# A second attention whose query and output products become three products of rounded parts, with keys and values loaded batch by batch

## The chip, the cores and the metric

The kernel runs on one core of one Trainium2 chip. The metric is the device time of one execution, in microseconds. Before the change three runs took 3955.93 to 3960.25 us, with a median of 3957.67 us.

## The reference, cut to what matters

The reference is two transformer layers over 8 batches of 512 tokens of 512 numbers, in fp32. Each layer is an attention and a mixture of 8 experts. The change touches only the second attention, which runs between the experts of layer 0 and the choice of experts of layer 1. It first builds its input x (the residual stream plus what the experts of layer 0 gave, times a gate) and then computes

```python
q = (x @ wq + bq).reshape(B, SQ, N_HEADS, D_HEAD)     # 16 heads of 32
k = (y @ wk + bk).reshape(B, SKV, N_HEADS, D_HEAD)    # 120 keys per batch
v = (y @ wv + bv).reshape(B, SKV, N_HEADS, D_HEAD)
scores = jnp.einsum('bqhd,bkhd->bhqk', q, k) / jnp.sqrt(D_HEAD)
attn = jax.nn.softmax(scores, axis=-1)
out = jnp.einsum('bhqk,bkhd->bqhd', attn, v).reshape(B, SQ, D_EMBED)
return out @ wo + bo
```

The input is layer-normed ahead of it. Its output, gated, is added to x, and a norm and a product with the gate weights give the logits for the second mixture. k and v were computed early in the kernel and lie in HBM (kT1, V1).

## The kernel before, in words

`attention1` is one block in which every engine has its own instruction stream, written out by hand. The 8 batches are taken in the order 4 to 7, 0 to 3 (ORDER). A body n handles batch n of that order in its core and parts of its neighbours: bodies run from -2 to 9. A body has 8 steps, one for each pair of a half of the heads and a tile of 128 tokens. For each step u

- TensorE (PE) makes the scores (L1861) into one of two double banks, transposes the softmax of step u-2 (L1871), and does the "fills" of the table FILLS1: other products which all go through only two PSUM banks, alternating. A fill waits until the fill two before it was emptied.
- VectorE (DVE) takes the maximum (L2029), subtracts it (L2033, `centre`), and after the exponential sums and inverts (L2038, L2041, `total`). Between these it normalizes tiles for the next batches (`norm` L2023, `norm3` L2060), adds the experts' results (`add`, L2009 and L2011, for the second four batches only, with their rows fetched by GpSimd's indirect DMA; L2014 is the statistics), and adds the attention's output to x (`result`, L2048, with statistics L2050, L2053).
- ScalarE (ACT) does the exponential (L1956), copies the transposes (L1951) and empties the fills: `yt` (transposed normed x, L1967), `q` (queries, L1969), `pv` (attention times values, L1976), `o` (output projection, L1973, into the tile `gated`, times the gate), `nt` (L1978). It also copies the keys of a batch (L1945).
- GpSimd (POOL) adds the biases (`bias` L1787, `residual` L1817), makes the inverse roots (L1803, L1805, L1811, L1813) and multiplies by the inverse sums (`share`, L1822).
- SP loads x a batch at a time (`load_x`, L1755), and stores x3 and out (L1771).

A fill `yt`, `nt` is 4 transposes; `pv` is 4 matmuls; a fill `q` (L1899) or `o` (L1909) is 4 matmuls of 128x512 in fp32, which appear in the trace as 8. The fills by step are

```python
FILLS1 = ((("q", 2), ("nt", 3), ("r", 2)),
          (("q", 3), ("yt", 0), ("r", 3)),
          (("pv", 2), ("yt", 1), ("pv", 3), ("yt", 2)),
          (("yt", 3), ("o", 0), ("q", 0)),
          (("o", 1),),
          (("o", 2), ("nt", 0)),
          (("o", 3), ("nt", 1), ("r", 0)),
          (("q", 1), ("pv", 0), ("pv", 1), ("nt", 2), ("r", 1)))
```

`r` is the product with the gate weights (L1917), whose result DVE takes (L2067). At the start, SP issues the loads of the first x, of wq, wo and gw, of the biases, of all keys and values, and then of the second batch's x. PE and ACT wait for all of the weights and biases first. `experts`, elsewhere in the kernel, already multiplies by rounded parts: ACT writes the weights rounded to fp32r (L1276), DVE writes what the rounding left (L1282), and three products are summed; so does the first attention for its q, k and v (L558).

Of the kernel before, what the change touches and what calls it, by code (L numbers as in the profile page):

```python
# [1664 lines left out]

BIAS1_AT = {0: (2, 0), 1: (2, 1), 5: (2, 2), 6: (2, 3)}
# [5 lines left out]
def attention1(nc, k, ins):  # L1672
    sems = Semaphores(nc)
    with ExitStack() as ctx:
        sb = lambda n, s, d=F32: ctx.enter_context(nc.sbuf_tensor("a1_" + n, s, d))
        sem = lambda n: sems.enter_context(nc.semaphore("a1_" + n))
        wq, wo, gw = sb("wq", [P, DC, D]), sb("wo", [P, DC, D]), sb("gw", [P, DC, E])
        bq = sb("bq", [P, DC])
        bv, bo, bf = sb("bv", [P, DC]), sb("bo", [P, D]), sb("bf", [P, D])
        kT, V = sb("kT", [P, DC, B * CL]), sb("V", [CL, B, D])  # L1680
        kcur = sb("kcur", [P, 2, DC, 2, CL])
        X, Y, G = sb("X", [P, 4, QT, D]), sb("Y", [P, QT, D]), sb("G", [P, 2, 2, D])
# [4 lines left out]
        xT, qT = sb("xT", [P, DC, S]), sb("qT", [P, DC, S])  # L1687
# [3 lines left out]
        OT, N3, N3T = sb("OT", [P, DC, S]), sb("N3", [P, 2, D]), sb("N3T", [P, 2, DC, P])  # L1691
        gated = sb("gated", [P, 2, D])
# [5 lines left out]
        w_in, kv_in, bf_in, folded, kzeroed = sem("weights_in"), sem("kv_in"), sem("bf_in"), sem("folded"), sem("kzeroed")  # L1698
        k_ready = sem("k_ready")
# [6 lines left out]
        r_biased, x3_ready = sem("r_biased"), sem("x3_ready")  # L1706
# [31 lines left out]

        comb = lambda i: i >= PLAIN
# [3 lines left out]
        with nc.Block() as block:  # L1743
            @block.sync
            def _(sp):
# [13 lines left out]
                for dst, src in ((wq, "wq1"), (wo, "wo1"), (gw, "gw1")):  # L1759
                    sp.dma_start(dst[:, :, :], ins[src].rearrange("(c p) n -> p c n", p=P)).then_inc(w_in, 16)  # L1760
                sp.dma_start(bq[:, :], ins["bq1"]).then_inc(w_in, 16)
                sp.dma_start(bo[:, :], ins["bo1"][None, :].to_broadcast([P, D])).then_inc(w_in, 16)
                sp.dma_start(bv[:, :], ins["bv1"]).then_inc(kv_in, 16)
                sp.dma_start(kT[:, :, :], k.kT1).then_inc(kv_in, 16)
                sp.dma_start(V[:, :, :], k.V1).then_inc(kv_in, 16)
                for n in bodies:
                    if 0 <= n - 1 < B:
# [5 lines left out]
                    if -2 <= n < B - 3:  # L1773
                        load_x(n + 3)
# [4 lines left out]
            def _(pool):  # L1779
# [63 lines left out]
            def _(pe):  # L1843
                pe.wait_ge(w_in, 16 * 5)

                def scores(n, s):
                    u, cp, t = STEPS1 * n + s, s // QT, s % QT
                    if s == 0:
                        pe.wait_ge(k_ready, n + 1)
# [3 lines left out]
                    if u == 0:  # L1853
                        pe.wait_ge(kv_in, 48)
# [21 lines left out]
                def do(n, f):  # L1876
# [14 lines left out]
                    if kind == "yt":  # L1891
                        pe.wait_ge(y_ready, QT * i + a + 1)
                        for c in range(DC):
                            mm = nc.tensor.transpose(m[:, c * P:c * P + P], Y[:, a, c * P:c * P + P], k.ident[:, :])
                    elif kind == "q":
                        for t in range(QT):
# [3 lines left out]
                    elif kind == "pv":  # L1900
                        pe.wait_ge(pt_out[a % 2], STEPS1 * i + QT * (a // 2) + QT)
                        for r in range(4):
                            mm = nc.tensor.matmul(m[DH1 * r:DH1 * r + DH1, :], V[:, ORDER[i], (4 * a + r) * DH1:(4 * a + r + 1) * DH1],
                                                  PT[0:CL, a // 2, 4 * (a % 2) + r, :], start=True, stop=True)
                    elif kind == "o":
                        for c in range(DC):
                            wait_emptied(pe, i, ("pv", c))
                        for c in range(DC):
                            mm = nc.tensor.matmul(m, OT[:, c, a * P:a * P + P], wo[:, c, :], start=(c == 0), stop=(c == DC - 1))  # L1909
# [24 lines left out]
            def _(act):  # L1934
                act.wait_ge(kzeroed, 1)
                act.wait_ge(w_in, 16 * 5)

                def keys(i):
                    if i == 0:
                        act.wait_ge(kv_in, 48)  # L1940
                    if i >= 2:
                        act.wait_ge(s_done, STEPS1 * (i - 1))
                    for r in range(4):
                        p = slice(DH1 * r, DH1 * r + DH1)
                        copy = act.activation(kcur[p, i % 2, :, r % 2, :], kT[p, :, ORDER[i] * CL:ORDER[i] * CL + CL], ACT.Copy)  # L1945
                    copy.then_inc(k_ready, 1)
# [11 lines left out]
                def empty(n, f):  # L1958
                    kind, a = f
                    if kind == "r" or not there(n, f):  # L1960
                        return
# [4 lines left out]
                    if kind == "yt":  # L1966
                        x = act.activation(xT[:, :, a * P:a * P + P], chunks(m), ACT.Copy)  # L1967
                    elif kind == "q":
                        x = act.activation(qT[:, a, :], m, ACT.Identity, bias=bq[:, a:a + 1])  # L1969
                    elif kind == "o":  # L1970
                        if QT * i + a >= 2:
                            act.wait_ge(x3_ready, QT * i + a - 1)
                        x = act.activation(gated[:, a % 2, :], m, ACT.Copy, scale=k.gate[:, 1:2])  # L1973
                    elif kind == "pv":

                        x = act.activation(OT[:, a, :], m, ACT.Identity, bias=bv[:, a:a + 1])  # L1976
# [3 lines left out]

                for n in bodies:
                    for s in range(STEPS1):
# [14 lines left out]
                        if s == 5 and 0 <= n + 1 < B:  # L1997
                            keys(n + 1)

            @block.vector  # L2000
            def _(dve):
# [17 lines left out]
                def norm(i, t):  # L2019
                    dve.wait_ge(rst, QT * i + t + 1)  # L2020
                    if i:
                        wait_filled(dve, i - 1, ("yt", t))
                    dve.tensor_scalar(Y[:, t, :], X[:, i % 4, t, :], mv[:, t, 0:1], rstd[:, t:t + 1], ALU.subtract, ALU.mult)\  # L2023
# [19 lines left out]
                def result(n, f):  # L2043
                    t, i = f[1], batch_of(n, f)
                    a, x = QT * i + t + 1, X[:, i % 4, t, :]
                    wait_emptied(dve, i, f)
                    dve.wait_ge(r_biased, a)
                    dve.tensor_tensor(x, x, gated[:, t % 2, :], ALU.add).then_inc(x3_ready, 1)  # L2048
                    dve.wait_ge(x3_ready, a)
# [18 lines left out]

                for n in bodies:
                    for s in range(STEPS1):  # L2070
                        u = STEPS1 * n + s
                        if softmax(n):
                            centre(u)
                        if s in NORM3_AT and 0 <= n - 1 < B:
                            norm3(n - 1, NORM3_AT[s])
                        if s in NORM1_AT and 0 <= n + NORM1_AT[s][0] < B:
                            norm(n + NORM1_AT[s][0], NORM1_AT[s][1])
                        if s in ADD_AT and 0 <= n + ADD_AT[s][0] < B:
                            add(n + ADD_AT[s][0], ADD_AT[s][1])
# [90 lines left out]
```

## Time and profile before

| | us |
|---|---|
| median of 3 runs | 3957.67 |
| the profiled execution | 3954.27 |
| its span, first to last instruction | 3952.5 |
| PE busy in the span | 3696.9 (94%) |
| DVE busy | 2928.8 (74%) |
| ACT busy | 1903.4 (48%) |
| POOL busy | 1092.4 (28%) |

The second attention runs from 2032.6 us of the span (its first instruction, a memset on POOL) to 2573.6 us (the last copy of logits). Busy shares are of the whole span; the matmuls' ends are modelled, so distances between starts say more of PE than durations do.

### The profile page before, as it was taken

How to read it: one execution, taken by the hardware profiler on the slowest of the kernel's cores; microseconds unless marked ns; L12 is line 12 of the kernel's file. 1: busy time of each engine (PE TensorE's matmuls, PEld its weight loads, DVE VectorE, ACT ScalarE, POOL GpSimd, SP SyncE). 2: the span in 40 equal slices, each digit the busy share in tenths (PEclk: the TensorE clock that was granted, in tenths of full speed). 3: DMA queues.
4: the chain of work that ended last, by engine and by line, in shares of the span. 5: the costliest groups of instructions: out<-in, count | busy, mean ns of one | idle time of the engine just before them, and what ended most of it. 6: DMA issues, size and time to landing. Idle time of an engine off the chain costs nothing. (4 is left out here: it accounts for less than half of the span.)

```text
span 3952.5 us, 62618 instructions
## 1 busy us (share of the span) xinstructions
PE 3696.9 (94%) x21884; PEld 2919.7 (74%) x21884; DVE 2928.8 (74%) x4545; ACT 1903.4 (48%) x2703; POOL 1092.4 (28%) x1008
## 2 busy tenths in 40 slices
PE   7899999999899999999969999849999999999998
PEld 4556666566479888899955555549999999999997
DVE  5567766676668788787627888678888788888885
ACT  2555655565445555554415444414444444444443
POOL 2222211222001111111025665313333334333332
PEclk9999999999899999999979999959999999999999
DMA  4000010100257787776640221126777777786774
GB/s 160 29 32 16 27 35 30 32 13 17 80 177 265 247 288 245 272 260 211 203 141 30 72 91 54 54 76 208 236 239 235 222 221 236 234 241 207 238 233 128
DMA packets 386958, 596.53 MB, mean 151 GB/s; under 512 B 26559, under 2 KB 192511, under 8 KB 386559
## 3 DMA queue, kind: packets, MB, share of 16 engines
q1 hardware_dynamic: 352575, 521.68, 39.5%
q0 software_dynamic: 24864, 58.54, 6.7%
q10 hardware_dynamic: 9368, 14.33, 1.0%
q8 instruction: 90, 1.47, 0.2%
q14 instruction: 61, 0.50, 0.0%
HBM read 535.36 MB, written 59.12 MB: 150 GB/s over the span
## 5 line engine op out<-in xcount | busy, mean ns | idle before, releaser
L1282 DVE TENSOR_TENSOR e_all<-e_all_raw,e_WH 128x2048 fp32r<-128x2048 f32 x240 | 545.3, 2289 | 36.2 <-ACT e_WH L1276 36.2
L1441 PE MATMUL bank<-e_xh,e_WH 128*128 128x256 f32 x1984 | 563.2, 284 | 9.6 <-DVE e_xl L1313 5.4
L1441 PE MATMUL bank<-e_xh,e_all 128*128 128x256 f32 x1984 | 562.1, 283 | 0.0
L1441 PE MATMUL bank<-e_xl,e_WH 128*128 128x256 f32 x1984 | 562.0, 283 | 0.0
L1276 ACT ACTIVATE e_WH<-e_all_raw 128x2048 fp32r<-128x2048 f32 x240 | 458.1, 1910 | 188.6 <-DMA e_all_raw<-in_w 188.4
L1494 PE MATMUL bank<-e_WH,e_hh 128*128 128x512 f32 x1192 | 473.5, 397 | 0.0
L1494 PE MATMUL bank<-e_WH,e_hl 128*128 128x512 f32 x1192 | 468.3, 393 | 0.0
L1441 PEld LDWEIGHTS bank<-e_xh,e_WH 128*128 128x128 f32 x1984 | 379.0, 191 | 14.8 <-issue 13.0
L1441 PEld LDWEIGHTS bank<-e_xl,e_WH 128*128 128x128 f32 x1984 | 379.0, 191 | 0.9
L1441 PEld LDWEIGHTS bank<-e_xh,e_all 128*128 128x128 f32 x1984 | 378.9, 191 | 0.0
L1517 ACT ACTIVATE e_sil<-bank 128x256 f32<-128x256 f32 x248 | 95.2, 384 | 366.2 <-PE bank L1441 365.5
L1441 PE MATMUL bank<-f_xh,f_wl 128*128 128x256 f32 x960 | 270.7, 282 | 0.0
L1243 POOL COPY e_icol<-idx 128x2 int32 (+1 forms) x64 | 60.9, 951 | 742.7 <-PE bank L1268 616.3
L1494 PEld LDWEIGHTS bank<-e_WH,e_hl 128*128 128x128 f32 x1192 | 223.8, 188 | 51.5
L1494 PEld LDWEIGHTS bank<-e_WH,e_hh 128*128 128x128 f32 x1192 | 223.9, 188 | 48.5
L672 ACT ACTIVATE a_Pr<-bank,a_nmax 128x632 f32<-128x632 f32 x256 | 201.1, 787 | 120.2 <-DVE a_nmax L786 113.7
L1257 POOL TENSOR_SCALAR e_veps<-e_mv 128x2 f32<-128x2 f32 x64 | 56.8, 888 | 660.5 <-DVE e_mv L1299 660.5
L679 ACT ACTIVATE a_PT<-bank 128x512 f32<-128x512 f32 x256 | 148.5, 593 | 173.0 <-PE bank L518 172.9
L1282 DVE TENSOR_TENSOR e_rest<-e_rest_raw,e_WH 128x2048 fp32r<-128x2048 f32 x72 | 164.8, 2289 | 84.0 <-ACT e_WH L1276 84.0
L1494 PE MATMUL bank<-e_all,e_hh 128*128 128x512 f32 x568 | 223.6, 394 | 0.0
L1441 PE MATMUL bank<-f_xh,f_wh 128*128 128x256 f32 x720 | 203.8, 283 | 2.2 <-ACTq L1504 2.2
L1441 PE MATMUL bank<-f_xl,f_wh 128*128 128x256 f32 x720 | 203.7, 283 | 0.0
(380 smaller groups left out, 9213.8 us busy)
## 6 DMA issues: line engine op xcount, KB each, us to landing
e_all_raw<-in_w SPq DMA_DIRECT2D x320, 512.0 KB, 4.5
f_wl_raw<-in_w SPq DMA_DIRECT2D x120, 1024.0 KB, 5.6
e_all_raw<-in_w SPq DMA_DIRECT2D x80, 1024.0 KB, 5.3
e_rest_raw<-in_w SPq DMA_DIRECT2D x72, 1024.0 KB, 5.4
f_X<-in_x SPq DMA_DIRECT2D x32, 256.0 KB, 2.6
f_R<-in_x SPq DMA_DIRECT2D x32, 256.0 KB, 4.1
x<-f_R SPq DMA_DIRECT2D x32, 256.0 KB, 2.0
a_X<-x SPq DMA_DIRECT2D x32, 256.0 KB, 3.4
```

What stands on the lines that cost most here:

```text
L672: act.activation(Pr[:, slot, :], Sb[r][:, 0:KEYS], ACT.Exp, bias=nmax[:, slot:slot + 1], accum_out=rsum[:, slot:slot + 1]).then_inc(exp_do ...
L679: act.activation(PT[:, r, 0:QT, qt * P:qt * P + P], chunks(ptb[bk]), ACT.Copy).then_inc(pt_out[bk], 1)
L1243: pool.tensor_copy(self.icol[:, 0:t.rm], self.idx_i[:, ds(t.chunk, t.rm)]).then_inc(self.icopied.sem, 1)
L1257: pool.tensor_scalar(self.veps[:, :], self.mv[:, :, 1], EPS, None, ALU.add).then_inc(self.veps_step.sem, 1)
L1276: act.activation(self.WH(p), self.raw(p), ACT.Copy).then_inc(self.high_ready.sem, 1)
L1282: dve.tensor_tensor(self.WL(p), self.raw(p), self.WH(p).bitcast(F32), ALU.subtract).then_inc(self.w_ready.sem, 1)
L1441: mm = nc.tensor.matmul(up[n % RING][:, q * ROWS:q * ROWS + ROWS], w, xx[:, c, :], start=(c == 0 and i == 0), stop=(c == DC - 1 and i == 2))
L1494: mm = nc.tensor.matmul(down[m], h, w, start=(f == 0 and i == 0), stop=(f == FC - 1 and i == 2))
L1517: act.activation(sil[:, n % 2, :], up[n % RING][:, 0:ROWS], ACT.Silu).then_inc(act_done.sem, 1)
```

## The change

- The fills `q` and `o` become 12 matmuls each: weights and inputs are split into a part rounded to fp32r and a rest, and three products (high by high, high by low, low by high) are summed in PSUM.
- For that, ACT writes the rounded part of a `yt` or `pv` fill (xTh, OTh), and DVE then writes the rest (`low`) from the same PSUM bank, which is free only after it. 8 such `low` per body: the first fill's follows `centre`, the middle fills' stand ahead of `total`, the last fill's behind it.
- The weights are split likewise: wq ahead of the bodies, wo at the start of body 0, on ACT and then DVE (128x2048 each).
- `result` takes the output projection from PSUM itself, times the gate, in one instruction; ACT's copy to `gated` is gone.
- Keys and values are loaded per batch by SP (`load_kv`, 5 DMAs), the keys straight to their place; ACT's 4 copies per body are gone. kT and V for all batches, and one Y tile of 4, are gone too.
- The first batch is biased, summed and normed ahead of the bodies, on POOL and DVE. SP loads its x, wq, its keys and values, then the second batch's x, and wo, gw and bo last; PE waits at each product for what it needs.

```diff
+YRING = 3
@@ SP
+                def load_kv(i):
+                    if i >= 2:
+                        sp.wait_ge(s_done, STEPS1 * (i - 1))
+                    for r in range(4):
+                        p = slice(DH1 * r, DH1 * r + DH1)
+                        sp.dma_start(kcur[p, i % 2, :, r % 2, :], k.kT1[p, :, ORDER[i] * CL:ORDER[i] * CL + CL]).then_inc(k_in[i % 2], 16)
+                    if i >= 2:
+                        wait_filled(sp, i - 2, ("pv", 3))
+                    sp.dma_start(V[:, i % 2, :], k.V1[:, ORDER[i], :]).then_inc(v_in[i % 2], 16)
...
-                            sp.wait_ge(x3_ready, QT * (n - 1) + t + 1)
+                            wait_emptied(sp, n - 1, ("o", t))
@@ PE
-                            mm = nc.tensor.matmul(m, wq[:, c, a * P:a * P + P], xT[:, c, :], start=(c == 0), stop=(c == DC - 1))
+                            wh, wl = (by_rows(w)[:, c, a * P:a * P + P] for w in (wqh, wql))
+                            for j, (w, x) in enumerate(((wh, xTh), (wh, xTl), (wl, xTh))):
+                                mm = nc.tensor.matmul(m, w, x[:, c, :], start=(c == 0 and j == 0), stop=(c == DC - 1 and j == 2))
...
@@ ACT
-                        x = act.activation(xT[:, :, a * P:a * P + P], chunks(m), ACT.Copy)
+                        act.activation(xTh[:, :, a * P:a * P + P], chunks(m), ACT.Copy).then_inc(kept_high, 1)
+                        return
...
-                        x = act.activation(gated[:, a % 2, :], m, ACT.Copy, scale=k.gate[:, 1:2])
...
+                weights_high(wqh, wq_raw, (wq_in, 48))
                 for n in bodies:
+                    if n == 0:
+                        weights_high(woh, wo_raw, (wo_in, 48))
@@ DVE
-                    dve.tensor_tensor(x, x, gated[:, t % 2, :], ALU.add).then_inc(x3_ready, 1)
+                    dve.scalar_tensor_tensor(x, mb[bk_], k.gate[:, 1:2], x, ALU.mult, ALU.add).then_inc(emptied[bk_], 1)
...
+                def low(n, f):
...
+                    dve.wait_ge(kept_high, high(i, f))
+                    if kind == "yt":
+                        part = slice(a * P, a * P + P)
+                        x = dve.tensor_tensor(xTl[:, :, part], chunks(mb[bk_]), xTh[:, :, part].bitcast(F32), ALU.subtract)
+                    else:
+                        x = dve.scalar_tensor_tensor(OTl[:, a, :], mb[bk_], bv[:, a:a + 1], OTh[:, a, :].bitcast(F32),
+                                                     ALU.add, ALU.subtract)
+                    x.then_inc(emptied[bk_], 1)
...
+                for t in range(QT + 1):
+                    if t < QT:
+                        add(0, t)
+                    if t:
+                        norm(0, t - 1)
+                weights_low(wql, wq_raw, wqh, 1)
                 for n in bodies:
...
+                        if n == 0 and s == 0:
+                            weights_low(wol, wo_raw, woh, 2)
                         if softmax(n):
                             centre(u)
+                        low(n, FILLS1[s][0])
...
+                        for f in FILLS1[s][1:-1]:
+                            low(n, f)
                         if softmax(n):
                             total(u)
                         for f in FILLS1[s]:
+                            if f == FILLS1[s][-1] and len(FILLS1[s]) > 1:
+                                low(n, f)
```

## Rows read from the trace of the kernel before

**Rows 1.** Busy time by stretch: start:end, length, PE, PEld, DVE, ACT, POOL, PEclk, DMA share, GB/s.
```profile
2035.00:2077.70 42.70, 13.71 (x32) 6.92 (x33) 11.60 (x20) 6.27 (x11) 20.50 (x25) 0.57 0.79 249
2077.70:2122.80 45.10, 38.41 (x176) 22.19 (x176) 33.55 (x44) 22.91 (x34) 23.74 (x21) 0.85 0.00 1
2122.80:2177.60 54.80, 53.26 (x272) 29.72 (x268) 43.87 (x61) 31.12 (x49) 34.06 (x35) 1.00 0.16 58
2177.60:2240.50 62.90, 57.52 (x289) 33.05 (x289) 54.48 (x70) 30.71 (x48) 36.77 (x39) 0.97 0.26 84
...
2368.50:2431.70 63.20, 57.53 (x289) 33.06 (x289) 56.32 (x72) 30.71 (x48) 38.12 (x41) 0.97 0.21 67
2431.70:2488.80 57.10, 55.63 (x289) 32.09 (x288) 42.08 (x58) 30.89 (x48) 26.45 (x25) 1.00 0.10 38
...
2534.05:2573.60 39.55, 33.05 (x177) 20.26 (x176) 15.10 (x32) 12.79 (x21) 8.98 (x13) 0.96 0.18 67
```

**Rows 2.** Timeline of body 4: start, us, engine, line, operation [idle before <-releaser].
```profile
2345.99 4.20 DVE L2048 TENSOR_TENSOR a_X<-a_X,a_gated 128x512 f32<-128x512 f32 x1
...
2346.61 1.28 POOL L1817 TENSOR_TENSOR a_X<-a_X,a_bo 128x512 f32<-128x512 f32 x1
...
2347.83 1.80 POOL L1822 TENSOR_TENSOR a_Pr<-a_Pr,a_rinv 128x960 f32<-128x960 f32 x1
...
2352.23 1.25 POOL L1787 TENSOR_TENSOR a_X<-a_X,a_bf 128x512 f32<-128x512 f32 x1
2352.28 1.16 DVE L2033 TENSOR_TENSOR a_Pr<-bank,a_smax 128x960 f32<-128x960 f32 x1
...
2355.11 1.60 PE L1917 MATMUL bank<-a_gw,a_N3T 128*128 128x8 f32 x8 [3.94 <-ACT a_gated L1973]
```

**Rows 3.** Timeline of PE, step 0 of body 4: scores, transposes, an fp32 fill `q`.
```profile
2304.35 1.08 PE L1861 MATMUL bank<-a_kcur,a_qT 64*128 64x240 f32 x8
2305.36 0.65 PE L1871 MATMUL bank<-ident,a_Pr 128*120 128x128 f32 x4
2305.85 3.60 PE L1899 MATMUL bank<-a_xT,a_wq 128*128 128x512 f32 x8
2309.28 0.60 PE L1871 MATMUL bank<-ident,a_Pr 128*120 128x128 f32 x4
```

**Rows 4.** Timeline of PE, first attention: first and last of 12 products of rounded parts.
```profile
530.37 0.48 PE L558 MATMUL bank<-f_wh,f_xh 128*128 128x512 f32 x1
...
533.21 0.60 PE L544 MATMUL bank<-ident,f_X 128*128 128x128 f32 x4
```

**Rows 5.** Groups by line, 1850 to 2600 us: count | busy us, mean ns | idle before.
```profile
L2033 DVE TENSOR_TENSOR a_Pr<-bank,a_smax 128x960 f32<-128x960 f32 x64 | 74.1, 1157 | 2.2
...
L1956 ACT ACTIVATE a_Pr<-a_Pr 128x960 f32<-128x960 f32 x64 | 64.3, 1004 | 104.6 <-DVE a_Pr L2033 104.3
...
L2048 DVE TENSOR_TENSOR a_X<-a_X,a_gated 128x512 f32<-128x512 f32 x32 | 56.8, 1776 | 14.2 <-ACT a_gated L1973 13.9
...
L1795 POOL DMA_INDIRECT a_G<-y,slot x32 | 33.6, 1050 | 7.6 <-issue 7.6
...
L2011 DVE SCALAR_TENSOR_TENSOR a_X<-a_G,w,a_X 128x512 f32<-128x512 f32 x16 | 12.0, 752 | 0.6
```

**Rows 6.** Groups by line, whole span: the splits of the experts.
```profile
L1313 DVE TENSOR_TENSOR f_xl<-bank,f_xh 128x512 fp32r<-128x512 f32 x39 | 27.0, 692 | 2.0
L1276 ACT ACTIVATE f_wh<-f_wl_raw 128x2048 fp32r<-128x2048 f32 x72 | 135.6, 1908 | 0.6 <-DMA f_wl_raw<-in_w 0.6
L1282 DVE TENSOR_TENSOR f_wl<-f_wl_raw,f_wh 128x2048 fp32r<-128x2048 f32 x72 | 163.8, 2285 | 7.0 <-ACT f_wh L1276 7.0
```

**Rows 7.** Timeline of the start of the second attention.
```profile
2061.61 1.26 POOL L1787 TENSOR_TENSOR a_X<-a_X,a_bf 128x512 f32<-128x512 f32 x1 [12.45 <-DMA a_X<-x]
...
2067.16 9.57 PE L1899 MATMUL bank<-a_xT,a_wq 128*128 128x512 f32 x16 [0.78 <-ACT a_xT L1967]
...
2078.83 1.16 DVE L2029 TENSOR_REDUCE a_smax<-bank 128x8 f32<-128x960 f32 x1 [9.13 <-PE bank L1861]
```

More of the change, by code:

```diff
@@ L1664 @@
 NORM3_AT = {4: 0, 5: 1, 6: 2, 7: 3}
+SPLIT1 = [f for f in FILL1_ORDER if f[0] in ("yt", "pv")]
+YRING = 3
 BIAS1_AT = {0: (2, 0), 1: (2, 1), 5: (2, 2), 6: (2, 3)}
@@ L1737, in turned_in, with high @@
             return u if 0 <= u < STEPS1 * B else None
+        def high(i, f):
+            n = len(SPLIT1) * (i + LATE.get(f, 1) + 2) + SPLIT1.index(f)
+            return sum(1 for m in range(n + 1) if there(m // len(SPLIT1) - 2, SPLIT1[m % len(SPLIT1)]))
         comb = lambda i: i >= PLAIN
@@ L1764, in _ @@
-                sp.dma_start(kT[:, :, :], k.kT1).then_inc(kv_in, 16)
-                sp.dma_start(V[:, :, :], k.V1).then_inc(kv_in, 16)
+                sp.dma_start(by_rows(wq_raw), ins["wq1"].rearrange("(c p) n -> p c n", p=P)).then_inc(wq_in, 16)
+                sp.dma_start(bq[:, :], ins["bq1"]).then_inc(wq_in, 16)
+                sp.dma_start(bv[:, :], ins["bv1"]).then_inc(wq_in, 16)
+                sp.wait_ge(kzeroed, 1)
+                load_kv(0)
+                load_x(1)
+                sp.dma_start(by_rows(wo_raw), ins["wo1"].rearrange("(c p) n -> p c n", p=P)).then_inc(wo_in, 16)
@@ L1893, in do @@
                         for c in range(DC):
-                            mm = nc.tensor.transpose(m[:, c * P:c * P + P], Y[:, a, c * P:c * P + P], k.ident[:, :])
+                            mm = nc.tensor.transpose(m[:, c * P:c * P + P], Y[:, (QT * i + a) % YRING, c * P:c * P + P], k.ident[:, :])
                     elif kind == "q":
+                        pe.wait_ge(w_ready, 1)
                         for t in range(QT):
@@ L1908, in do @@
                         for c in range(DC):
-                            mm = nc.tensor.matmul(m, OT[:, c, a * P:a * P + P], wo[:, c, :], start=(c == 0), stop=(c == DC - 1))
+                            oh, ol = (o[:, c, a * P:a * P + P] for o in (OTh, OTl))
+                            for j, (o, w) in enumerate(((oh, woh), (oh, wol), (ol, woh))):
+                                mm = nc.tensor.matmul(m, o, by_rows(w)[:, c, :], start=(c == 0 and j == 0), stop=(c == DC - 1 and j == 2))
                     elif kind == "nt":
@@ L1934, in _, with weights_high @@
             def _(act):
[L1935 to L1946, printed above, removed]
+                def weights_high(to, raw, there):
+                    act.wait_ge(*there)
+                    act.activation(to[:, :], raw[:, :], ACT.Copy).then_inc(w_high, 1)
                 def keep_turned(u, i):
@@ L1959, in empty @@
                     kind, a = f
-                    if kind == "r" or not there(n, f):
+                    if kind in ("o", "r") or not there(n, f):
                         return
@@ L2067, in logits, with weights_low @@
                     dve.tensor_copy(k.logits[:, ORDER[i] * QT + t, :], mb[bk_][:, 0:E]).then_inc(emptied[bk_], 1)
+                def weights_low(to, raw, top, n):
+                    dve.wait_ge(w_high, n)
+                    dve.tensor_tensor(to[:, :], raw[:, :], top[:, :].bitcast(F32), ALU.subtract).then_inc(w_ready, 1)
+                def low(n, f):
+                    kind, a = f
+                    i = batch_of(n, f)
+                    if kind not in ("yt", "pv") or not there(n, f):
+                        return
+                    bk_, c_ = fill(i, f)
+                    dve.wait_ge(kept_high, high(i, f))
[6 more added lines that the diff above has]
+                    x.then_inc(emptied[bk_], 1)
+                for t in range(QT + 1):
+                    if t < QT:
+                        add(0, t)
+                    if t:
+                        norm(0, t - 1)
+                weights_low(wql, wq_raw, wqh, 1)
                 for n in bodies:
```

78 lines of the change are left out of this document (41 added, 37 removed).

## The prediction

> **What bounds the kernel now.** I read the table of 40 slices first: PE is the busy engine nearly everywhere, so I went to the one stage that the change touches, from 2032.6 to 2573.6 us, and cut it by body, at each body's first scores [rows 1]. The reader is to see three kinds. The plain bodies (1, 6) take 54.8 and 57.1 us with PE busy for 53.3 and 55.6: PE is the bound. The four bodies 2 to 5, in which the experts' results are added, run from 2177.60 to 2431.70, 254.1 us or 63.5 each, with PE busy for 57.5 in the two shown, though their products are those of body 6 (x289 in both). DVE is busy for 56.3 of 63.2 there, against 42.1 of 57.1. And the start, 42.7 us, has PE busy for a third.
>
> The timeline of body 4 says what the extra 6.4 us are [rows 2]. DVE's `result` (L2048, both inputs in SBUF) begins at 2345.99 and takes 4.20 us. It ends 0.56 us after POOL's L1822 (2347.83 + 1.80): it stood still while POOL worked on L1817 and L1822. The same instruction of DVE reading a bank, L2033, is not held up: at 2352.28 it takes 1.16 beside POOL's L1787, and its mean over 64 is 1157 ns [rows 5]. L2048's mean is 1776, against 0.69 for a 128x512 operation [rows 6]. Everything on DVE moves back, the exponential and ACT's copy L1973 behind it too, and PE has waited 3.94 us for that copy when it starts L1917 at 2355.11.
>
> **The change part by part.**
>
> *The products.* A fp32 fill takes 2309.28 - 2305.85 = 3.43 us [rows 3]; 12 products of rounded parts take 533.21 - 530.37 = 2.84 [rows 4]. PE saves 0.59 per fill, 64 fills, 38 us. This is no gain by itself: in the plain bodies only 8 x 0.59 = 4.7 of 57.1 would come out, and only if nothing else takes PE's place.
>
> *DVE's added work.* 8 `low` per body at 0.69 [rows 6] = 5.5 us. Taken off: in bodies 2 to 5, the standstill of L2048, since `result` now reads a bank, as L2033 does. 32 x (1.776 - 0.692) = 34.7 us in all [rows 5, 6], nearly all of it in these four bodies, some 8 us each. So DVE's busy time goes from 56.3 to about 54 there, and from 42.1 to 47.6 in the plain ones [rows 1]. DVE isn't the sole bound in either, but nearly in the first.
>
> *The new order of waits.* What decides is how the two take turns. PE's fills have two banks; that of a `yt` or `pv` fill was free after ACT's copy, and now waits for DVE as well, which is in the middle of `centre` (2.3 us) or `add` (two of L2011's kind and statistics, 2.5 us). I lay out one plain body from the durations of the rows, from its first scores at 0: PE 1.0 for scores, 0.5 per transpose group [rows 3], 2.8 per fill `q` or `o` [rows 4]; DVE 2.3 for `centre`, 1.3 for `total`, at least 1.1 between them for ACT's exponential (1004 ns) [rows 5], 1.6 for `result`, 0.9 for `add` without experts, 0.7 for `low`.
> - Steps 0 and 1: PE-bound, 6.2 us each, 6.9 before. Step 1's `yt` is emptied by ACT only at 12.4 (behind the exponential and `q`), so `low` ends at 13.1 and `total` at 14.4.
> - Step 2: PE is there at 12.5, DVE begins `centre` at 14.5. The fills `pv` 3 and `yt` 2 wait for the `low` of the two ahead of them: step 3 begins at 20.2, 7.7 us instead of 6.1.
> - Step 3 ends when `q` 0 does, which waited for the `low` of `yt` 3 at 25.2: 28.2, 8.0 us against 9.3.
> - Steps 4 and 5: PE-bound, 10.0 against 11.4. Step 6: the `o` 2 bank is free at 41.1, `o` 3 ends at 43.9, and the bank of `o` 3 must be emptied by `result`, behind `centre` 6 and `total` 6: step 7 begins at 48.5, 10.3 against 7.4.
> - Step 7: exponential, `q`, `low`, `low`, then `nt` and `r`: 9.5, body end 58.0.
>
> So a plain body takes 58.0 where body 6 took 57.1: +0.9. Body 1 lacks three fills of step 0 and 1 and takes 56.3: +1.5. With the experts' `add` (1.6 us longer) steps 2 and 7 grow, to 58.6. To this POOL adds: in steps 5 and 6 it has L1787, two L1795 at 1.05, L1817 and L1822, over 6 us a step beside the roots [rows 2, 5], and it holds up `norm3` by about 1.2: 59.8 each, four bodies 239.2, 14.9 less than 254.1. Body 0, now without the long waits for weights but with six `low` in a stretch that DVE bounds: +2.3. Body 7: +0.3. The last stretch: ACT's copy ahead of `result` goes and four fills are shorter, four `low` stand in the chain: -1.2. Bounds of all this: if no fill ever waited for a `low`, the bodies with experts would take DVE's busy time, 54.5, the plain ones PE's, 52; if every `low` were in the chain, 5.5 more per body than now, 254.1 - 34.7 + 22 for the four and +5.5 for the others. The laid-out value lies between, and I take it.
>
> *The start.* DVE's first maximum is at 2078.83, and POOL waited 12.45 us for the second batch's x, which stood behind all keys and values in SP's queue, until 2061.61 [rows 7]. By the shapes that x is now asked for behind 2.8 MB, not 7.2, and the first batch's chain does not wait for it: POOL's stream (1.26 + 0.8 per tile, four tiles) puts the last norm at 48 of the 2000s, DVE's split of wq (2.29) ends at 50.5 [rows 6], two `add` and four `low` with PE's transposes at the low clock bring `q` 0 to 57.5, against 2067.16. Two fills, half at the low clock as then (0.57 in this stretch [rows 1]), end at 65.6, scores at 66.6. There the added part comes: ACT's split of wo, 1.91, then DVE's, 2.29, ahead of the first `centre`: 2070.8, or 8.0 us earlier. Bounds: 12.2 if that split were hidden, 0 if x arrived as late as before.
>
> *Keys and values* per batch, 5 DMAs by SP: issued a body ahead of their use, DMA is busy for 0.10 to 0.26 of these stretches [rows 1]; at nothing. Uncovered, a few us per body. ACT's copies (2.4 us per body) were in ACT's idle time: nothing. SP's stores wait behind `load_kv` until `pv` 3 of step 2, and are needed from step 3 on: nothing.
>
> **The sum**: -8.0 + 2.3 + 1.5 - 14.9 + 0.9 + 0.3 - 1.2 = -19.1 us. The stages behind are unchanged. The profiled execution took 3954.27, so 3935.2; that execution is 3.4 under the median of the three runs, against which I give 3938.5.
>
> **The rivals.**
> *A, the turns cost less:* DVE runs ahead of PE more than I laid out, and the bodies with experts take 54.5, the plain ones 53, the start gives 10: 254.1 - 218 = 36, plus 6, plus 10: 3906. For: the scores and exponentials have spare buffers. Against: the fills have two banks only.
> *B, the turns eat the rest:* each body is 2.5 us longer than laid out (two more `low` and an `add` in the chain), 8 x 2.5 = 20: 3958, no change. For: DVE waited 13.9 us in all even for L1973's short copy [rows 5], and POOL's hold on `norm` is uncertain.
> *C, PE's clock (the slower side):* PE now idles in every body. Granted clock and busy share go together in the rows: 1.00 at 97% busy, 0.97 at 91%, 0.85 at 85% (body 0) [rows 1]. After the change PE has 52 us of work at full clock in some 59. If the clock fell to 0.75 through the bodies, this work would take 69, 10 more than laid out, 80 in all: 4018. It decides from 52 / 0.84 = 62 us on, that is below a mean clock of 0.84; just slower than before. Against it: body 5, at 91% busy with a hole of 4 us, kept 0.97. The Trainium skill, page "TensorE: Matmul & The Clock Gate", section "A second HAM failure mode: psum-queue depth-cycling", says that many short idles between groups of matmuls, when they cycle through banks, suffice to make the gate fall and rise again. No row here shows it with short idles alone; by that rule C would come true.
> *D, products of rounded parts gain nothing beside fp32 ones:* then the saving of 0.59 is gone where PE bounds, steps 0, 1, 4, 5 of each body, some 2.5 us each: 3958 too. The rows of the first attention, where both stand side by side, speak against it.
>
> **How the numbers follow.** Mine 0.54 (its own range 3920 to 3950), A 0.18, B and D 0.18, C 0.10. What can be told from no change is 0.2%, 7.9 us: faster means under 3949.8, slower over 3965.6. Faster: mine and A, 0.72; same 0.18; slower 0.10. The range leaves out nearly all of C (0.09) and the far sides of A and B (0.08): 3903 to 3962.
>
> **What would show it.** Right: the standstill of `result` is gone (under 0.8 us each); the four bodies take 58 to 61; the plain ones 57 to 59, no shorter than before; PE waits for DVE's `low` at `pv` 3 and `yt` 2 of step 2, and for `result` at `r` 0 of step 6; first maximum near 2071. Wrong: plain bodies of 53 (A), of 60 and more (B), a clock under 0.85 in the bodies (C), fills of 3.4 (D), or a wait of SP's loads that PE sees at a body's first scores.

## The result and the profile after

The changed kernel takes 3977.78 us (median of 5 runs, 3976.34 to 3979.14) against 3957.67: a ratio of 1.0052, 95% interval 1.0040 to 1.0064. It is slower by 20 us, where 19 us less were forecast, and lies above the range of 3920 to 3950 of my own forecast and above the whole range of 3903 to 3962. The profiled execution took 3978.66, its span 3976.8 us (3952.5 before). The mean granted clock is 0.963 (0.970 before).

The same cuts as in [rows 1], at each body's first scores; the last runs from the last scores to the copy of logits. The two rows behind it are cuts of body 4 that the text below uses. Columns as there.

```profile
2035.00:2067.90 32.90, 11.63 (x42) 8.70 (x42) 17.47 (x25) 5.72 (x8) 20.36 (x25) 0.57 0.73 234
2067.90:2117.50 49.60, 35.19 (x194) 24.20 (x194) 36.97 (x47) 22.09 (x31) 23.43 (x20) 0.86 0.02 6
2117.50:2178.90 61.40, 53.23 (x306) 38.49 (x302) 49.44 (x72) 26.28 (x40) 30.85 (x32) 0.92 0.18 60
2178.90:2244.20 65.30, 56.37 (x321) 41.92 (x320) 52.87 (x78) 26.32 (x40) 38.69 (x40) 0.90 0.28 89
2374.10:2439.00 64.90, 54.83 (x321) 40.64 (x321) 55.39 (x81) 26.30 (x40) 39.64 (x40) 0.92 0.24 73
2439.00:2499.90 60.90, 54.06 (x321) 40.26 (x320) 45.44 (x67) 26.39 (x40) 24.15 (x24) 0.94 0.11 40
2547.50:2594.70 47.20, 38.36 (x193) 28.83 (x192) 16.85 (x33) 10.59 (x17) 7.16 (x13) 0.76 0.14 54
2331.50:2336.20 4.70, 4.70 (x21) 3.65 (x22) 4.04 (x6) 1.19 (x2) 2.55 (x3) 0.51 0.00 0
2336.20:2342.30 6.10, 6.10 (x29) 4.73 (x28) 4.75 (x8) 2.06 (x3) 2.46 (x3) 1.00 0.18 69
```

The reader is to see that the start is shorter by 10 us, that every body behind it is longer, and that PEclk, 0.97 to 1.00 in [rows 1] for bodies 1 to 6, is 0.90 to 0.94. Against the terms of the sum (changes against the kernel before, in the distances between first scores, us; e3 is the changed kernel with added work for PE, below; "all behind" begins at L1052, the first instruction that reads the logits):

| stretch | forecast | measured | with fillers (e3) |
|---|---|---|---|
| start and body 0 | -5.7 | -5.3 | -4.9 |
| body 1 | +1.5 | +6.6 | +3.0 |
| bodies 2 to 5 | -14.9 | +6.0 | -7.4 |
| body 6 | +0.9 | +3.8 | +3.7 |
| body 7 | +0.3 | +2.4 | +3.2 |
| last stretch | -1.2 | +7.7 | +3.8 |
| all behind | 0 | +3.1 | +2.8 |

Of the plain body 6 the steps are 6.24, 6.23, 7.64, 9.62, 4.83, 5.26, 10.20, 10.89 us. Laid out were 6.2, 6.2, 7.7, 8.0, 4.8, 5.2, 10.3, 9.5. Six of eight stand within 0.1 us, the new waits included; steps 3 and 7 are 1.6 and 1.4 longer. Why, PE's timeline of body 4 shows, from the end of step 2 into step 3. (The lines of the changed kernel are L1925 for `yt`, L1938 for `pv`, L1892 for the scores, L1902 for the transposed softmax, L1933 for `q`, L1948 for `o`, L1952 for `nt`, L1956 for `r`; on DVE, L2113 and L2115 are `low`, L2079 is `result`, L2091 `norm3`.)

```profile
2325.26 0.60 PE L1925 MATMUL bank<-ident,a_Y 128*128 128x128 f32 x4
2328.01 1.07 PE L1938 MATMUL bank<-a_PT,a_V 120*32 120x512 f32 x8 [2.15 <-DVE a_OTl L2115]
2331.50 1.12 PE L1925 MATMUL bank<-ident,a_Y 128*128 128x128 f32 x4 [2.42 <-DVE a_xTl L2113]
2332.55 1.97 PE L1892 MATMUL bank<-a_kcur,a_qT 64*128 64x240 f32 x8
2334.45 1.11 PE L1902 MATMUL bank<-ident,a_Pr 128*120 128x128 f32 x4
2335.35 0.99 PE L1925 MATMUL bank<-ident,a_Y 128*128 128x128 f32 x4
2336.18 0.60 PE L1902 MATMUL bank<-ident,a_Pr 128*120 128x128 f32 x4
```

The two waits for `low` are where the forecast had them, at `pv` 3 and `yt` 2. Behind them the scores take 1.97 us, where they took 1.08 [rows 3], and the transposes 1.11 for 0.65. PE is at 1.2 GHz: the granted clock from 2331.50 to 2336.20 is 0.51, and 1.00 behind it (the last two rows of the table of cuts). At 2336.18 it is back at 2.4 GHz. The same at the turn from step 6 to 7, all engines:

```profile
2354.51 0.71 DVE L2079 SCALAR_TENSOR_TENSOR a_X<-bank,gate,a_X 128x512 f32<-128x512 f32 x1
2354.82 1.29 POOL L1846 TENSOR_TENSOR a_X<-a_X,a_bo 128x512 f32<-128x512 f32 x1
2355.27 0.50 PE L1948 MATMUL bank<-a_woh,a_OTh 128*128 128x512 f32 x1 [1.21 <-DVE a_X L2079]
...
2358.74 1.50 DVE L2091 TENSOR_SCALAR a_N<-a_X,a_mv,a_rstd 128x512 f32<-128x512 f32 x1 [0.27 <-POOL a_rstd L1842]
...
2361.45 0.71 DVE L2079 SCALAR_TENSOR_TENSOR a_X<-bank,gate,a_X 128x512 f32<-128x512 f32 x1
...
2362.22 1.06 PE L1956 MATMUL bank<-a_gw,a_N3T 128*128 128x8 f32 x8 [3.02 <-DVE a_X L2079]
...
2363.21 1.77 PE L1892 MATMUL bank<-a_kcur,a_qT 64*128 64x240 f32 x8
```

`result` is L2079 now. Its standstill is gone: 0.71 us beside POOL's L1846, where L2048 took 4.20 [rows 2]. But the bank of `o` 3 is emptied only by it, behind `norm3` (L2091, itself held to 1.50) and `total`, so that r 0 waits 3.02 us, and the scores behind it take 1.77. All of bodies 1 to 6 have a slow start of step 3 (scores of 1.97) and of step 7 (1.15 to 1.80). The groups, 1850 to 2620 us:

```profile
L1956 PE MATMUL bank<-a_gw,a_N3T 128*128 128x8 f32 x256 | 36.7, 271 | 20.3 <-DVE a_X L2079 18.1 <-DVE a_OTl L2115 1.2 <-ACT a_qT L2000 1.0
L1938 PE MATMUL bank<-a_PT,a_V 120*32 120x512 f32 x256 | 35.2, 645 | 16.8 <-DVE a_OTl L2115 13.8 <-DVE a_xTl L2113 1.4 <-ACT a_qT L2000 1.3
L2115 DVE SCALAR_TENSOR_TENSOR a_OTl<-bank,a_bv,a_OTh 128x512 fp32r<-128x512 f32 x32 | 23.8, 748 | 24.0 <-ACT a_OTh L2003 23.3
L2079 DVE SCALAR_TENSOR_TENSOR a_X<-bank,gate,a_X 128x512 f32<-128x512 f32 x32 | 23.1, 723 | 7.2 <-PE bank L1948 7.1
L2113 DVE TENSOR_TENSOR a_xTl<-bank,a_xTh 128x512 fp32r<-128x512 f32 x32 | 21.5, 673 | 9.2 <-ACT a_xTh L1997 9.0
```

The terms of DVE were right: 748 and 673 ns for a `low` (0.69 forecast), 723 for `result` (1776 before [rows 5]). The start was near, by DVE's timeline: the first maximum at 2071.78 (forecast 2070.8, before 2078.83 [rows 7]), directly behind the split of wo. The split of wq took 3.35 us, though, where 2.29 were laid out.

```profile
2049.80 3.35 DVE L2102 TENSOR_TENSOR a_wql<-a_wql_raw,a_wqh 128x2048 fp32r<-128x2048 f32 x1
...
2069.57 2.29 DVE L2102 TENSOR_TENSOR a_wol<-a_wol_raw,a_woh 128x2048 fp32r<-128x2048 f32 x1 [7.86 <-ACT a_woh L1976]
...
2071.78 1.15 DVE L2059 TENSOR_REDUCE a_smax<-bank 128x8 f32<-128x960 f32 x1
```

### The profile page after: what moved, and what is told of

Its sections match the earlier page's. It is cut to its first block and busy times, and to the rows that moved or that the text cites. A ratio compares the mean times of both kernels' runs of the same rounds, so it can differ in the third digit from the quotient of the medians.

```text
span 3976.8 us, 63203 instructions
## 1 busy us (share of the span) xinstructions
PE 3682.7 (93%) x22140; PEld 2986.6 (75%) x22140; DVE 2945.9 (74%) x4611; ACT 1872.8 (47%) x2641; POOL 1070.6 (27%) x1008
## 5 line engine op out<-in xcount | busy, mean ns | idle before, releaser
L1243 POOL COPY e_icol<-idx 128x2 int32 (+1 forms) x64 | 50.8, 794 | 719.2 <-PE bank L1268 591.3
```

Source lines behind the costliest of these rows:

```text
L1243: pool.tensor_copy(self.icol[:, 0:t.rm], self.idx_i[:, ds(t.chunk, t.rm)]).then_inc(self.icopied.sem, 1)
```

## The experiments

Each ran beside the kernel before, on the same chip as it (3956.29 for e1 to e4, 3956.54 for e5, e6, e8 and e9, 3956.56 for e7, e10 and e11, 3955.21 for e12), and each ratio is to that. "Body 4" is its length in the profiled execution. e4, e6, e9 and e12 leave out part of the arithmetic, and the fillers compute nothing of use: these are measuring tools and not versions to keep.

| | us | ratio to before, 95% interval | body 4 |
|---|---|---|---|
| before | 3957.67 | | 64.2 |
| after | 3977.78 | 1.0052 (1.0040 to 1.0064) | 64.9 |
| e1 direct result alone | 3948.98 | 0.9983 (0.9974 to 0.9993) | 61.2 |
| e2 after, fp32, no split | 3932.97 | 0.9942 (0.9925 to 0.9958) | 61.2 |
| e3 after, fillers | 3952.08 | 0.9990 (0.9980 to 0.9999) | 61.3 |
| e4 after, `low` kept, fp32 products | 3998.93 | 1.0106 (1.0089 to 1.0123) | 68.3 |
| e5 e2, r 0 later | 3919.52 | 0.9908 (0.9892 to 0.9925) | 58.3 |
| e6 after, no `low` | 3919.64 | 0.9906 (0.9890 to 0.9923) | 59.0 |
| e8 after, r 0 later | 3964.75 | 1.0023 (1.0013 to 1.0032) | 62.8 |
| e9 `low` without the bank | 3962.67 | 1.0017 (1.0007 to 1.0026) | 61.8 |
| e12 the bank held, no `low` | 3965.68 | 1.0023 (1.0013 to 1.0033) | 62.1 |
| e10 e8, fillers | 3952.84 | 0.9993 (0.9984 to 1.0002) | 62.9 |
| e11 e1, fillers | 3944.59 | 0.9972 (0.9963 to 0.9982) | 59.5 |
| e7 e5, `result` of o 3 earlier | 3913.16 | 0.9889 (0.9874 to 0.9904) | 57.8 |

**e1, the direct result alone**, in the kernel before:

```diff
-                    dve.tensor_tensor(x, x, gated[:, t % 2, :], ALU.add).then_inc(x3_ready, 1)
+                    dve.scalar_tensor_tensor(x, mb[bk_], k.gate[:, 1:2], x, ALU.mult, ALU.add).then_inc(emptied[bk_], 1)
```

> The kernel before with one edit: result on DVE takes the o bank from PSUM, times the gate, and ACT's copy to gated is gone. Theory 'standstill': the four bodies with the experts' add lose the 4 us holes of L2048 and fall from 63.5 to about the 57.1 of the plain body, 3957.7 - 26 = 3932. Rival 'the holes move' (the norms or adds, which also read SBUF, stand behind POOL instead): 3950 to 3958.

The time lies between the two theories: the four bodies with experts go from 254.1 to 242.8 us, but bodies 1 and 6 grow from 54.8 and 57.1 to 58.1 and 58.7, and the whole gains 7.3, not 26. PE's timeline of body 4 has the wait and the clock of after, without any `low`:

```profile
2349.58 0.60 PE L1913 MATMUL bank<-ident,a_N 128*128 128x128 f32 x4
2352.53 1.06 PE L1917 MATMUL bank<-a_gw,a_N3T 128*128 128x8 f32 x8 [2.35 <-DVE a_X L2045]
2353.52 1.61 PE L1861 MATMUL bank<-a_kcur,a_qT 64*128 64x240 f32 x8
2355.06 1.11 PE L1871 MATMUL bank<-ident,a_Pr 128*120 128x128 f32 x4
2355.96 4.29 PE L1899 MATMUL bank<-a_xT,a_wq 128*128 128x512 f32 x8
```

**e2 and e4, the split taken apart.** e2 is after with the fp32 weights, inputs and products of the kernel before, without `low` and without the splits of wq and wo; the loads, the first batch ahead and the direct `result` stay. e4 keeps every split and `low`, and makes each fill `q` and `o` one fp32 product of the rounded parts; the products with the rests are left out.

```diff
-                            wh, wl = (by_rows(w)[:, c, a * P:a * P + P] for w in (wqh, wql))
-                            for j, (w, x) in enumerate(((wh, xTh), (wh, xTl), (wl, xTh))):
-                                mm = nc.tensor.matmul(m, w, x[:, c, :], start=(c == 0 and j == 0), stop=(c == DC - 1 and j == 2))
+                            mm = nc.tensor.matmul(m, by_rows(wqh)[:, c, a * P:a * P + P].bitcast(F32), xTh[:, c, :].bitcast(F32), start=(c == 0), stop=(c == DC - 1))
```

> The changed kernel without the rounded parts: fp32 products for q and o, ACT alone empties yt and pv, no low on DVE; the loads by batch, the first batch first and the direct result stay. Theory 'turns' (what is lost is lost by the low between PE and its two banks): the start gives 10 beyond the direct result, near 3922, that is 55 us under the changed kernel. Rival 'the loads or the shorter Y ring cost': nearer to 3945 or more.

> The changed kernel with all its low and splits, but q and o as one fp32 product of the rounded parts (8 instructions of 0.43 us instead of 12 of 0.23); the product of the rests is left out. It prices the products alone. If PE is the bound in most steps: 64 x 0.6 = 38 us more, 4016. If the turns bound steps 2, 6 and 7: some 20 to 25 more, 4000. If a denser PE keeps its clock and hides it: 3978 to 3985.

e2 came 11 us above its theory; e4 lies where steps 2, 6 and 7 are bound by the turns.

**e6** leaves the rests at zero: 12 products as in after, no `low` in the bodies, and ACT's copy frees the bank.

```diff
-                        act.activation(xTh[:, :, a * P:a * P + P], chunks(m), ACT.Copy).then_inc(kept_high, 1)
-                        return
+                        x = act.activation(xTh[:, :, a * P:a * P + P], chunks(m), ACT.Copy)
```

> The changed kernel with 12 products of rounded parts, but without the low of yt and pv on DVE (the rests are zeros, written once), so ACT alone frees their banks. It is the fourth corner: fp32 without low 3933, fp32 with low 3999, rounded with low 3978. If the two are independent, low costs 66 and the products give 21: 3912. Theory 'turns': without low PE is nearer to being the bound, the products give their full 64 x 0.6 = 38: 3895. Rival 'the wait for result at r 0 holds': 3915 to 3920.

The four make a square. Without `low`: fp32 3932.97, rounded 3919.64. With it: fp32 3998.93, rounded 3977.78. The products give 13 and 21 us, of the 38 of their arithmetic; the rests cost 66 and 58. The two sides that start at e2 (13 and 66) are not clean, for e2 lacks the splits of the weights too; the clean ones are 21 for the products and 58 for the rests. e6 came out where its rival had it, "the wait for result at r 0 holds", and its trace has that wait, 16.8 us in six places, as after has.

**e9 and e12** tell what of a `low` costs: its time in DVE's order, or the bank that it holds. In both the rests are zero as in e6. In e9 each `low` is an equally long statistics instruction at the same place, reading SBUF, and ACT frees the bank; only `q` 0 and `o` 0 still wait for the last of these instructions. In e12 it is a copy of 8 columns, which frees the bank.

```diff
-                        x = dve.tensor_tensor(xTl[:, :, part], chunks(mb[bk_]), xTh[:, :, part].bitcast(F32), ALU.subtract)
...
+                    dve.bn_stats(idle6[:, high(i, f) - 1, :], wqh[:, 0:D].bitcast(F32)).then_inc(kept_high, 1)
# e12 instead:
+                    dve.tensor_copy(k.logits[:, ORDER[i] * QT + a, :], mb[bk_][:, 0:E]).then_inc(emptied[bk_], 1)
```

> The changed kernel with the rests as zeros, where each low is replaced by a 0.69 us operation on DVE (bn_stats of constant data in SBUF) at the same place with the same wait, but ACT frees the bank; q 0 and o 0 wait for the last of them. It tells the hold of the banks from DVE's added work. Theory 'hold': within 10 us of the run without low. Theory 'DVE's load': within 10 us of the changed kernel, 3968 to 3978.

> The changed kernel with the rests left at zero, and at the place of each low only a copy of 8 columns from its bank on DVE (142 ns, the logits' copy), which frees the bank as low did. It has the hold on the banks without DVE's 0.7 us each. In the traces the attention ends 26 us later with DVE's time and without the hold (e9 against e6), and 27 us later again with both (the changed kernel). If the two add up, this one ends 24 to 30 us behind e6: 3944 to 3950. If the hold costs only what DVE's added time makes of it (rival), it costs less than 15: 3922 to 3934. If the hold is all of it, 3965 and more.

By their medians neither met the forecasts: e9 lies between its two, and e12 is 3965.68 where 3944 to 3950 were expected if the parts add up, and 3965 and more if the hold is all of it. But behind the attention, where nothing was changed, e9 and e12 spent 1392 and 1391 us, e6 1379 and after 1381, which I can't explain. So I compare the attention alone, in the profiled executions, from its first instruction (a memset on POOL) to the first that reads the logits (L1052): 512.4 us in e6, 536.5 in e9, 540.1 in e12, 563.2 in after (542.1 before). DVE's time without the bank costs 24 us, the bank without the time 28, both 51: they about add up. These are single executions, and e6's was 4.2 us above its median; if the medians are taken, less what each spent more than e6 behind the attention, the three are 30, 34 and 56. By either, a `low` costs about half by what it takes, half by what waits for its turn.

**e3, the clock.** Filler matmuls of 128x512 into a bank that is free then, results unused, run in PE's waits of after; they wait only for ACT's copy out of that bank, and everything else stays.

```diff
+                SPIN = {("pv", 3): 5, ("yt", 2): 5, ("r", 0): 8, ("nt", 2): 8}
...
+                            if n >= 1 and u is not None and f in SPIN and (f[0] != "nt" or n == B - 1):
+                                spin(u, SPIN[f])
```

> The changed kernel with idle PE time filled: 5 matmuls of 128x512 on constant data (about 1.2 us) ahead of pv 3 and of yt 2 in step 2, 8 ahead of r 0 in step 6, 8 ahead of nt 2 in the last body; they write a transpose bank that was copied. Their results are not used. Theory 'clock' (about 3 us per body are PE at 1.2 GHz after its waits): granted clock from 0.92 to near 1 in the bodies, 3977.8 - 3 x 7 - some of the end = 3945 to 3957. Theory 'turns' alone: no gain, 3978 to 3985, as the filling delays the waiting fills a little.

More work for PE makes the kernel 25.7 us faster in the medians (20.2 in the spans; its profiled execution was 6 above its median). First its body 4 in the windows, then PE's timeline at the place shown of after; L1962 is the filler.

```profile
2299.50:2360.80 61.30, 55.40 (x339) 41.03 (x338) 55.65 (x81) 26.18 (x40) 39.70 (x40) 1.00 0.31 95
```

The timeline:

```profile
2315.54 0.60 PE L1925 MATMUL bank<-ident,a_Y 128*128 128x128 f32 x4
2315.90 1.40 PE L1962 MATMUL bank<-a_wqh 128*128 128x512 f32 x5
2318.30 1.07 PE L1938 MATMUL bank<-a_PT,a_V 120*32 120x512 f32 x8 [1.00 <-DVE a_OTl L2124]
2319.30 1.43 PE L1962 MATMUL bank<-a_wqh 128*128 128x512 f32 x5
2321.79 0.66 PE L1925 MATMUL bank<-ident,a_Y 128*128 128x128 f32 x4 [1.07 <-DVE a_xTl L2122]
2322.38 1.08 PE L1892 MATMUL bank<-a_kcur,a_qT 64*128 64x240 f32 x8
```

The waits for DVE end no sooner: `pv` 3 and `yt` 2 start 18.81 and 22.30 us behind the body's first scores in both kernels. The scores take 1.08 again and PEclk is 1.00. Steps 3 and 7 are 8.07 and 9.48 us: the 8.0 and 9.5 laid out. The fillers don't keep the clock everywhere: body 6 gains nothing (60.8 for 60.9), for its step 0 ran at the low clock instead and took 9.13, as step 0 of bodies 2, 3 and 7 took 7.8.

**e5 and e8, r 0 later**: the fill r 0 goes to the head of step 7, in e2 and in after, so that PE doesn't stand ahead of the scores for `result`.

```diff
-          (("o", 3), ("nt", 1), ("r", 0)),
-          (("q", 1), ("pv", 0), ("pv", 1), ("nt", 2), ("r", 1)))
+          (("o", 3), ("nt", 1)),
+          (("r", 0), ("q", 1), ("pv", 0), ("pv", 1), ("nt", 2), ("r", 1)))
```

> The kernel of the run without the split, with the fill r 0 moved from the end of step 6 to the head of step 7, and its logits copied ahead of total there. In that run PE stood before r 0 for the bank of o 3, which result holds behind centre and total (step 6 is 9.5 us, 7.4 before), and ran step 7 at the low clock in the bodies of 10.8 (9.2 before). Theory 'the bank of o 3 and the clock after it': steps 6 and 7 together lose 2 to 3 us in each of 7 bodies, 3933 - 18 = 3915. Rival 'DVE is late anyway' (the wait moves to scores or q 1 of step 7): 3930 to 3935.

> The changed kernel with r 0 at the head of step 7, as above. If the low clock after that wait is worth 1.5 us a body and the wait itself 1: 3978 - 7 x 2.5 = 3960. If DVE is late anyway: 3975 to 3980.

Both gain 13 us, a little less than e5's theory and e8's had. In e5, step 6 falls to 6.09 and step 7 grows to 11.06. In e8 the two are 6.73 and 13.53: r 0 still waits 1.4 us in step 7, with the low clock behind it, and `nt` 2 waits another 1.0 to 1.1 for a `low`.

**e10** adds e3's fillers to e8 (6 ahead of r 0), **e11** two fp32 fillers ahead of r 0 to e1 (below), **e7** puts `result` of `o` 3 ahead of `total` in e5.

```diff
+                            if n >= 1 and u is not None and f == ("r", 0):
+                                spin(u, 0, 2)
```

> The changed kernel with r0 moved to the head of step 7 (3964.8 alone) and with filler matmuls (results unused) in PE's waits: 5 before pv 3, 5 before yt 2, 6 before r 0, 8 before nt 2 of the last body. If the clock is what the waits cost (theory), this takes back what the fillers took back without the move, some 25 us: 3938 to 3944, with granted clock 1.00 in the bodies. If the waits for DVE themselves set the time (rival), fillers change nothing here: 3962 to 3968.

e10 missed: 3952.84, no better than e3. Step 3 is 8.07 as hoped, but step 7 is 13.5 to 14.5 in bodies 2 to 5. r 0 no longer waits, and `nt` 2 waits 2.40 instead of 1.0 for the same `low`; that wait had no filler, and the clock fell behind it (step 0 of the next body 7.8 to 8.7, for 6.23). PE's timeline of body 5:

```profile
2421.10 0.66 PE L1952 MATMUL bank<-ident,a_N 128*128 128x128 f32 x4 [2.40 <-DVE a_OTl L2126]
```

Step 7 is no shorter with PE at full clock in its first part, which points to DVE's order as its bound with r 0 moved. That e3 and e10 end at the same time need not mean the same bound: e10 didn't keep its clock.

> The kernel before with the direct result (3949.0 alone), and 2 filler matmuls of fp32 (results unused) before r 0 of step 6, where PE waited 2.35 us for the result. Clock theory: step 6 stays at 9.5 us, step 7 of bodies 2 to 5 goes from 10.8 to about 9.2, so 6 us less: 3941 to 3945. Rival, step 7 is long since DVE's stream is late there: step 7 keeps 10.8 and the time 3947 to 3952.

e11 is the clean one, without splits. PE's timeline at the place shown of e1:

```profile
2345.40 1.88 PE L1923 MATMUL bank<-a_wq 128*128 128x512 f32 x4
2347.92 1.06 PE L1917 MATMUL bank<-a_gw,a_N3T 128*128 128x8 f32 x8 [0.64 <-DVE a_X L2052]
2348.91 1.08 PE L1861 MATMUL bank<-a_kcur,a_qT 64*128 64x240 f32 x8
2349.92 0.65 PE L1871 MATMUL bank<-ident,a_Pr 128*120 128x128 f32 x4
2350.41 3.60 PE L1899 MATMUL bank<-a_xT,a_wq 128*128 128x512 f32 x8
```

Step 6 stays at 9.5, step 7 goes from 10.82 to 9.19 in bodies 3 to 5 (body 2 had 9.19 already) and from 10.87 in body 1. The median falls by 4.4, as the clock theory had it. In e1 the wait at r 0 is 2.35 us in bodies 2 to 5 alike, yet step 7 was long in bodies 3 to 5 only.

> fp32 products, direct result, keys and values per batch, r 0 at the head of step 7 (3919.5 alone), and now the result of o 3 ahead of total in step 6. Theory: r 0's wait of 0.8 us and the step behind it shrink, but total is 1.6 us later and with it the turn of step 7: 3914 to 3920. Rival, the softmax chain is what step 7 waits for: 3922 to 3930.

3913.16, a little under what was expected, and 1.1% under before: the best version found, with fp32 products and without any split. Its body 4 takes 57.8 us (64.2 before, 64.9 after), and body 5 is, in the windows:

```profile
2335.40:2393.20 57.80, 55.76 (x289) 31.82 (x288) 50.84 (x73) 26.18 (x40) 39.78 (x40) 1.00 0.28 85
```

PE is busy for 96% of it at full clock.

## Why the prediction was wrong

*Right:* what bounded the kernel before; the start and body 0 (-5.3 for -5.7, though the start gave 7.1 for 8.0 and body 0 behind it lost 1.7 for 2.3, so that two small errors cancel); the durations of `low` and of the direct `result`; the places of the new waits; and the layout of a plain body, six steps of it in after, the other two (8.07 and 9.34) in e3.

*The step that failed* is the price of PE's clock, in rival C. The sum has no term for it, because it was priced as a mean over the body's work: 52 us at full clock in 59, so that by this reckoning a loss is hidden down to a mean clock of 0.88, and makes the kernel slower than before only below 0.84. The mean came to 0.90 to 0.94, and it cost all the same. The clock is at 1.2 GHz right behind the waits, for 4.7 us in step 3 of body 4 and for some 3.5 in its step 7, and just there PE is the chain: DVE waits for the scores that it makes. Body 6 lost 3.0 us so in steps 3 and 7, all that it is above the layout. The row that should have told me stood among mine: L1917 behind the hole of 3.94 us took 1.60 [rows 2], and 1.06 at full clock. The next row of PE's timeline of before, which I left out, is

```profile
2356.64 1.97 PE L1861 MATMUL bank<-a_kcur,a_qT 64*128 64x240 f32 x8
```

Before had one such place per body with experts (and two in body 0); after has two in each of bodies 1 to 6. e3 gives it back by work that is of no use: in its profiled execution 13.5 us in bodies 2 to 5, 3.6 in body 1, 3.9 in the last stretch, with small changes elsewhere 20 of the miss of 43 between the spans (24.3 longer, where 19.1 shorter was forecast). The rule cited in C was weighed too low. The Trainium skill, page "TensorE: Matmul & The Clock Gate", section "A second HAM failure mode: psum-queue depth-cycling", has the clock fall and rise with short idles between groups that cycle through banks; the traces of after and e1 agree, with waits of 1.0 to 3.02 us.

*The second, smaller:* the layout of a body with experts, 59.8. With the clock back it is 61.3 to 62.1, 7.5 us over it in four bodies. Step 2 is 9.1 to 10.1 us there against 7.7 in a plain body: the experts' `add` stands between the two `low` and stretches both waits. I had added 0.6 a body for it. That the order of the `low` and `add` is what stretches the step is read from the timeline; no run changed it. Step 6 is 10.8 for 10.2, and there POOL adds to it: L2091 takes 1.50 where POOL reads beside it, 0.54 where not.

*The third:* the last stretch. Four `low` behind one another in a chain with nothing beside them, and the clock at 0.76 (0.96 before [rows 1]), cost +7.7, where -1.2 was forecast; 3.8 stay with the fillers. PE's timeline:

```profile
2553.94 0.66 PE L1952 MATMUL bank<-ident,a_N 128*128 128x128 f32 x4 [2.47 <-DVE a_OTl L2115]
2554.60 1.88 PE L1956 MATMUL bank<-a_gw,a_N3T 128*128 128x8 f32 x8
...
2567.39 1.93 PE L1938 MATMUL bank<-a_PT,a_V 120*32 120x512 f32 x8 [1.59 <-DVE a_OTl L2115]
2571.01 0.77 PE L1948 MATMUL bank<-a_woh,a_OTh 128*128 128x512 f32 x1 [1.69 <-DVE a_OTl L2115]
```

*Where the expected gain went.* The standstill was worth 34.7 us of DVE's time by the forecast (L2048's 56.8 us became L2079's 23.1), and e1 shows 7.3 of the whole's: the copy by ACT had freed the bank of `o` 3 early; the direct `result` holds it until DVE comes, PE waits there, and the clock falls. e11 takes back 4.4 of that by fillers, e5 13.4 by moving r 0. The loads and the first batch ahead, on the other hand, are worth 16 us between e1 and e2 in the medians; the first scores come 18 us sooner (2079.6, 2061.5). After has them at 2067.9, 6 us later than e2. That is the first batch's `low` and not the splits of the weights: in after PE waits 8.63 us for the first of these `low` (L2113), which stand behind the split of wq in DVE's order, and e6, with both splits but without `low`, needs 28.5 us from the first instruction of the attention to its first scores, e2 29.5, after 35.2.

*Rivals.* A is out. B happened too, in part: it gave 2.5 us a body over the layout for `low` and `add` in the chain; bodies 2 to 5 are 5.2 over it, and 1.9 with the clock back. D is out: where PE bounds, steps 0 and 4 took 6.24 and 4.83 us for 6.87 and 5.47. C happened in part: the kernel is slower than before, by a clock that in the bodies never came near the 0.75 with which C was priced. It had 0.10.

*Open:* the time behind the attention, where the code is the same. It is 1377.5 to 1379.5 us in before, e1, e2, e5, e6, e7 and e11, 1380.6 to 1381.4 in after, e3, e4, e8 and e10, and 1391 to 1392 in e12 and e9 (span less the start of L1052). 3 us of the miss lie there. No version with the `low` at other places was run, and none with the splits and e7's order of `result`.

## What to carry to other kernels

An operation put on a second engine between a product and the next use of its PSUM bank costs more than its duration, for the bank also waits for its place in that engine's order: here 64 operations of 0.7 us, 45 us in all on an engine that was busy for 74% of the span, cost 58 us, about half of it by the hold on the bank alone. Price a new wait of TensorE by the wait and by what runs at 1.2 GHz behind it, where that work is what the others wait for (here some 3 us a body); a mean clock over the stretch hides it. When a copy that frees a bank early is removed, look at who waits for the bank, and move that fill behind work that is ready: with that and one move on VectorE, a gain of 23 us (e2) became one of 43 (e7). Both are without the rounded parts: no version here made these pay, and only with fillers was the changed kernel not slower than before.

## What was not expected of the hardware

- PE's clock fell behind waits of 2.15 to 3.02 us amid steps that are busy otherwise (scores 1.77 to 1.97 us for 1.08), with mean clocks of 0.90 to 0.94 over the bodies that don't look like much. The length of the wait alone doesn't tell: in e1 a wait of 2.35 was followed by a step 7 of 9.19 us in body 2 and of 10.82 in bodies 3 to 5; waits of 1.0 to 1.2 us were mostly followed by full speed, but in body 6 of after waits of 1.28 and 1.01 in step 2 were followed by scores of 1.97, and in e3 one of 1.08 ahead of body 6 was.
- Filler matmuls in the waits, 18 per body from body 1 on and 8 more at the end, made a kernel faster by 25.7 us.
- The gain of three products of rounded parts over one fp32 product is 0.6 us per fill, in the steps that PE bounds (6.24 for 6.87 us), and was 13 to 21 us of 38 in the whole.
- A two-input operation of DVE from SBUF was held by POOL: the split of wq took 3.35 us beside POOL's L1816, that of wo 2.29 with POOL idle. With one input in PSUM (L2079, L2113, L2115), means of 673 to 748 ns show no such hold. The Trainium skill, page "SBUF — State Buffer", section "Who interferes with whom", says so of two inputs in SBUF. L2091, a `tensor_scalar`, has one such input and was held as well (1.50 us for 0.54); the same section says that `tensor_scalar` can enter a mode that takes both ports and then contends with GpSimd, which these times fit, though no run here shows the mode itself.
